# A sorted mixture-of-experts stage: its fp32 down product as three products of rounded halves

## The reference

```python
scores = sigmoid(x @ gate_w)                       # 32 experts
topk_w, topk_i = top_k(scores, 6); topk_w /= sum(topk_w)
combine = sum(one_hot(topk_i, 32) * topk_w[..., None], axis=1)
g = einsum('td,edf->tef', x, wg)                   # 256 -> 96 per expert
u = einsum('td,edf->tef', x, wu)
act = silu(g) * u
routed = einsum('tef,efd,te->td', act, wd, combine)  # 96 -> 256 per expert
```

## Time and profile before

| | us |
|---|---|
| median of three runs | 1384.87 (1383.31 to 1386.27) |
| span of the profiled execution | 1381.9 |
| TensorE busy | 1291.0 (93%) |
| ScalarE busy | 858.4 (62%) |
| VectorE busy | 844.4 (61%) |
| GpSimd busy | 617.0 (45%) |
| `sorted_tiles`: first transpose to last copy out | 608.6 to 955.1 |
| its down product, line 2018, 448 matmuls | 139.3 busy |

### The profile page before, as it was taken

How to read it: one execution, slowest core, us unless ns; L and a number is a source line. 1 busy time by engine, 2 the same in 40 slices (tenths; PEclk the granted TensorE clock), 3 DMA queues, 4 the chain that set the end, 5 groups by cost and what they waited for, 6 DMA issues and landing times. The chain is left out here.

```text
span 1381.9 us, 24599 instructions
## 1 busy us (share of the span) xinstructions
PE 1291.0 (93%) x7384; PEld 959.9 (69%) x7385; DVE 844.4 (61%) x3207; ACT 858.4 (62%) x2326; POOL 617.0 (45%) x542
## 2 busy tenths in 40 slices
PE   4999769999999999969999999997999999999997
PEld 3666446767777667757788888886667767777765
DVE  4587678777777677723333333333777777777774
ACT  1455427776677577635556656664777777777673
POOL 1111117777775777710000000001888888887820
PEclk9899979999999999999999999998999999999999
DMA  9977653333327422259976666664565665765510
GB/s 342 392 281 275 253 228 114 101 106 111 115 98 256 162 95 92 85 155 316 329 232 188 188 183 190 188 186 126 100 92 87 129 99 90 132 104 89 97 28 31
DMA packets 147284, 223.28 MB, mean 162 GB/s; under 512 B 13846, under 2 KB 128214, under 8 KB 142294
## 3 DMA queue, kind: packets, MB, share of 16 engines
q1 hardware_dynamic: 99350, 157.72, 33.9%
q0 software_dynamic: 36864, 53.50, 18.9%
q10 hardware_dynamic: 10944, 10.49, 2.6%
HBM read 105.27 MB, written 116.39 MB: 160 GB/s over the span
## 5 line engine op out<-in xcount | busy, mean ns | idle before, releaser
L1523 POOL DMA_INDIRECT l_sums<-sorted_y,slot_no x192 | 300.1, 1563 | 424.7 <-DMA l_sums<-base_dram 366.9
L1068 POOL DMA_INDIRECT sorted_x<-f_xn_row,slot_no x192 | 204.7, 1066 | 49.2 <-issue 44.5
L1224 ACT ACTIVATE f_prob<-f_prob,f_negmax 128x512 f32<-128x512 f32 (+3 forms) x256 | 142.6, 557 | 121.3 <-DVE f_negmax L1297 110.8
L2075 DVE SCALAR_TENSOR_TENSOR act_f<-hidden,rows_in,ps 128x96 f32<-128x96 f32 x224 | 70.5, 315 | 231.1 <-ACT hidden L2038 231.0
L1676 ACT ACTIVATE l_prob<-l_prob,l_negmax 128x512 f32<-128x512 f32 (+3 forms) x256 | 141.7, 555 | 104.9 <-DVE l_negmax L1760 97.2
L2000 PE MATMUL ps<-wgu_sb,xt_e 128*128 x896 | 184.2, 328 | 0.5 <-issue 0.4
L1565 PE MATMUL ps<-l_kt,l_qt 128*128 128x512 f32 (+3 forms) x512 | 170.5, 447 | 5.4 <-DVE l_qt L1751 4.8
L1127 PE MATMUL ps<-kt_s,f_qt 128*128 128x512 f32 (+3 forms) x512 | 170.8, 448 | 5.0 <-DVE f_qt L1288 4.4
L1297 DVE CUSTOM_DVE_ANT_0 f_prob<-ps,mask_add 128x512 f32<-128x512 f32 (+3 forms) x256 | 121.0, 486 | 83.5 <-issue 82.5
L1760 DVE CUSTOM_DVE_ANT_0 l_prob<-ps,mask_add 128x512 f32<-128x512 f32 (+3 forms) x256 | 121.0, 486 | 81.0 <-issue 79.7
L2000 PEld LDWEIGHTS ps<-wgu_sb,xt_e 128*128 128x128 f32 x896 | 139.9, 190 | 3.0 <-issue 2.0
(11 more groups left out here) (194 smaller groups left out, 2660.6 us busy)
## 6 DMA issues: line engine op xcount, KB each, us to landing
sorted_x<-zeros SPq DMA_DIRECT2D x14, 2304.0 KB, 9.8
rows_in<-sorted_x SPq DMA_DIRECT2D x112, 288.0 KB, 3.1
sorted_y<-rows_out SPq DMA_DIRECT2D x112, 256.0 KB, 2.1
wgu_sb<-in_wgu SPq DMA_DIRECT2D x16, 384.0 KB, 5.2
x_in<-in_x SPq DMA_DIRECT2D x8, 512.0 KB, 10.3
xn_dram<-xn SPq DMA_DIRECT2D x8, 512.0 KB, 4.0
base_dram<-x_in SPq DMA_DIRECT2D x8, 512.0 KB, 2.9
nqt_dram<-nqt_out SPq DMA_DIRECT2D x8, 512.0 KB, 3.9
```

The lines of the kernel that those rows point to most:

```text
L1068: pool.indirect_dma_start(sorted_x, bass.IndirectOffsetOnAxis(ap=slot_no[:, t, k:k + 1], axis=0), xn_row[buf][:], None).then_inc(scattered ...
L1224: act.activation(prob[:, i, qt, 0:w], prob[:, i, qt, 0:w], ACT.Exp, bias=negmax[:, i, qt:qt + 1], scale=-1.0, accum_out=rowsum[:, g // 2 % ...
L1523: pool.indirect_dma_start(sums[n % NSUM][:, t, :], None, sorted_y, bass.IndirectOffsetOnAxis(ap=slot_no[:, TT * GROUPS[n] + t, k:k + 1], a ...
```

## The change

The down product of line 2018 becomes `product3` on split halves. For that:

- `at` becomes a pair `at_hi`, `at_lo`. VectorE copies the turned activation to `at_hi` (rounded), waits for that copy on a semaphore of its own, and then subtracts: `at_lo` = PSUM - `at_hi`. `at_copied`, for which TensorE waits, is now counted up by the subtraction.
- The down weights become `wd_hi`, `wd_lo`. Chunks are loaded into two raw buffers in turn. VectorE splits chunk 0 at the start of the block, GpSimd splits chunks 1 to 7. The load of chunk n waits until raw buffer n%2 has been split. TensorE waits for the split of a chunk before the first down product that may use it.
- `ZCOLS`, the width of the zero tile from which `sorted_x` is cleared, is halved (each fill then reads it twice as often), and two small routing tensors live shorter. Both free SBUF.

```diff
-ZCOLS = 2304
+ZCOLS = 1152
...
-        sp.dma_start(self.wd[:, part, :], wd[:, part, :]).then_inc(self.chunk_loaded[n], 16)
+        sp.dma_start(self.wd_raw[n % 2][:], wd[:, part, :]).then_inc(self.wd_loaded[n % 2], 16)
...
                     if i == 0 and d % 2 == 0 and weights.EARLY + d // 2 < weights.CHUNKS:
-                        weights.load_chunk(sp, weights.EARLY + d // 2, wgu, wd)
+                        n = weights.EARLY + d // 2
+                        if n == 2:
+                            sp.wait_ge(wd_first, 1)
+                        else:
+                            sp.wait_ge(wd_split, n - 2)
+                        weights.load_chunk(sp, n, wgu, wd)
...
+        @block.gpsimd
+        def _(pool):
+            pool.wait_ge(wd_hi_made, 1)
+            for n in range(1, weights.CHUNKS):
+                part = slice(n * EACH, (n + 1) * EACH)
+                pool.wait_ge(wd_loaded[n % 2], 16 * (n // 2 + 1))
+                pool.tensor_copy(wd_s[0][:, part, :], wd_raw[n % 2][:]).then_inc(wd_hi_made, 1)
+                pool.wait_ge(wd_hi_made, n + 1)
+                pool.tensor_tensor(wd_s[1][:, part, :], wd_raw[n % 2][:], wd_s[0][:, part, :].bitcast(F32), ALU.subtract)\
+                    .then_inc(wd_split, 1)
...
-                        pe.matmul(y_ps[1 - par], at[1 - par][:],
-                                  wd_sb[:, bass.ds(owner, 1), :].rearrange("p a h -> p (a h)"), start=True, stop=True)\
+                        if c == 0:
+                            pe.wait_ge(wd_first, 1)
+                        elif c % EACH == 0 and c // EACH < weights.CHUNKS:
+                            pe.wait_ge(wd_split, c // EACH)
+                        product3(pe, y_ps[1 - par], [a[:] for a in at_s[1 - par]],
+                                 [w[:, bass.ds(owner, 1), :].rearrange("p a h -> p (a h)") for w in wd_s], True, True)\
                           .then_inc(y_ready, 1)
...
+            dve.wait_ge(wd_loaded[0], 16)
+            dve.tensor_copy(wd_s[0][:, 0:EACH, :], wd_raw[0][:]).then_inc(wd_hi_made, 1)
+            dve.wait_ge(wd_hi_made, 1)
+            dve.tensor_tensor(wd_s[1][:, 0:EACH, :], wd_raw[0][:], wd_s[0][:, 0:EACH, :].bitcast(F32), ALU.subtract)\
+               .then_inc(wd_first, 1)
...
                         dve.wait_ge(at_ready, c + 1)
-                        dve.tensor_copy(at[par][:], at_ps[par]).then_inc(at_copied, 1)
+                        dve.tensor_copy(at_s[par][0][:], at_ps[par]).then_inc(at_hi, 1)
+                        dve.wait_ge(at_hi, c + 1)
+                        dve.tensor_tensor(at_s[par][1][:], at_ps[par], at_s[par][0][:].bitcast(F32), ALU.subtract)\
+                           .then_inc(at_copied, 1)
```

More of the change, by code:

```diff
@@ L95, in build @@
         comb = sb("comb", [P, NT, NE])
-        slot_of = sb("slot_of", [P, NT, NE])
-        slot_top = sb("slot_top", [P, NT, 8])
         slot_no = sb("slot_no", [P, NT, TOPK], I32)
@@ L108, in build @@
                       xn_dram, base_dram, nqt_dram, nkv_dram, kt_dram, wq_dram, wvo_dram, rope_dram, sorted_x, tile_expert,
-                      comb, slot_of, slot_top, slot_no, ident, owner, owner_stored, mask, done, ps, weights, wgu, wd)
+                      comb, slot_no, ident, owner, owner_stored, mask, done, ps, weights, wgu, wd)
         with ExitStack() as ctx:
@@ L119, in attention @@
               xn_dram, base_dram, nqt_dram, nkv_dram, kt_dram, wq_dram, wvo_dram, rope_dram, sorted_x, tile_expert,
-              comb, slot_of, slot_top, slot_no, ident, owner, owner_stored, mask, done, ps, weights, wgu, wd):
+              comb, slot_no, ident, owner, owner_stored, mask, done, ps, weights, wgu, wd):
     def sb(name, shape, dt=F32):
@@ L148, in attention @@
     tile_c = latents(nc.sbuf_tensor("tile_c", [P, 1], F32))
+    slot_of = latents(nc.sbuf_tensor("slot_of", [P, NT, NE], F32))
+    slot_top = latents(nc.sbuf_tensor("slot_top", [P, NT, 8], F32))
     earlier = latents(nc.sbuf_tensor("earlier", [P, P], BF16))
@@ L855, in __init__ @@
         self.wgu = [whole.sb(f"wgu_sb{kc}", [P, NE, 2 * FE]) for kc in range(KC)]
-        self.wd = whole.sb("wd_sb", [FE, NE, H])
+        self.wd_hi = whole.sb("wd_hi", [FE, NE, H], F32R)
+        self.wd_raw = [ctx.enter_context(nc.sbuf_tensor(f"wd_raw{i}", [FE, self.EACH, H], F32)) for i in range(2)]
+        self.wd_loaded = [sem(f"wd_loaded{i}") for i in range(2)]
         self.rows_in = [ctx.enter_context(nc.sbuf_tensor(f"rows_in{i}", [P, 2, HW], F32)) for i in range(self.AHEAD)]
@@ L1896, in sorted_tiles @@
     AHEAD, EACH = weights.AHEAD, weights.EACH
-    rows_in, wgu_sb, wd_sb, expert_row = weights.rows_in, weights.wgu, weights.wd, weights.expert_row
+    rows_in, wgu_sb, expert_row = weights.rows_in, weights.wgu, weights.expert_row
     in_loaded, chunk_loaded, expert_loaded = weights.in_loaded, weights.chunk_loaded, weights.expert_loaded
     OUT = 4
+    wd_raw, wd_loaded = weights.wd_raw, weights.wd_loaded
+    wd_s = [weights.wd_hi, sb("wd_lo", [FE, NE, H], F32R)]
+    wd_hi_made, wd_first, wd_split = sem("wd_hi_made"), sem("wd_first"), sem("wd_split")
     rows_out = [sb(f"rows_out{i}", [P, 2, H]) for i in range(OUT)]
@@ L1903, in sorted_tiles @@
     act_f = [sb(f"act_f{i}", [P, FE]) for i in range(2)]
-    at = [sb(f"at{i}", [FE, P]) for i in range(2)]
+    at_s = [[sb(f"at_hi{i}", [FE, P], F32R), sb(f"at_lo{i}", [FE, P], F32R)] for i in range(2)]
     ALL_LAST = sum((NE - 1) << 8 * k for k in range(4))
@@ L1915, in sorted_tiles @@
     gu_ready, silu_done, act_done = sem("gu_ready"), sem("silu_done"), sem("act_done")
-    at_ready, at_copied = sem("at_ready"), sem("at_copied")
+    at_ready, at_hi, at_copied = sem("at_ready"), sem("at_hi"), sem("at_copied")
     y_ready, y_copied = sem("y_ready"), sem("y_copied")
@@ L1996, in steps @@
                         if c % EACH == 0 and c // EACH < weights.CHUNKS:
-                            pe.wait_ge(chunk_loaded[c // EACH], 16 * (KC + 1))
+                            pe.wait_ge(chunk_loaded[c // EACH], 16 * KC)
                         for kc in range(KC):
```

## The result

| | us |
|---|---|
| kernel after, median of 4 runs | 1400.48 (1399.87 to 1400.98) |
| kernel before, beside it, median of 4 | 1385.57 (1383.31 to 1386.49) |
| ratio, 95% interval | 1.0112 [1.0096, 1.0127] |
| span of the profiled execution | 1398.9 after 1381.9 |

The change costs 15 us in the timed runs and 17.0 us in the profiles. I had forecast 8.0 on the span, so the sign was right and the size was about half of what came. First the stage itself, busy time by stretch after the change; the row answers to the earlier trace rows.

A forecast was written before the change was run, and what follows sets the result against it. TensorE bounds the sorted experts' second part, hiding a loop by 0.02 us a tile; the loop takes over. Span 1381.9 + 4 (loop) + 2 (reads) + 2 (weights) = 1389.9, plus 3.0 to the median: 1393; range 1385 to 1403.

The forecast's parts named there:

- The loop: Sorted experts, 700 to 956 us: subtraction lengthens the two-tile round through the other engines from 2.79 to 3.03 us; +4 us.
- The reads: Sorted experts: TensorE's reads of expert numbers mostly hide in its new waiting; +2 us, bounds 0 and +13.7.
- the third row of the table: Stretch from copy out 65 to the last, 159 steps: forecast +5.5 us, from the +4 and +2 for 171 tiles.
- the reads stay on top of the loop: Rival, sorted experts: expert-number reads add fully to the longer round, 1.60 us a tile, +17.6, total 1404.5; chance 0.12.
- The zero tile: Fills that clear sorted_x, before the experts: halved width means more, shorter descriptors; forecast to cost nothing.
- That cover makes it nothing: Fills before the experts: GpSimd's scatter, waiting for them, ends 17 us before the first row is turned; cost 0.
- The weights: Start of the sorted experts: splitting weight chunks delays SyncE's chunk 2 by up to 2.2 us; +2, bounds 0 and +8.
- the first part: Sorted experts, 608 to 700 us, bound by DMA at 1.74 us a tile; the slower 1.52 us pace hidden there.
- the other estimate: GpSimd's copy when splitting a weight chunk: 0.9 us by the skill's line-rate rule, in place of 1.5.
- The halt of 3 us at chunk 4: SyncE, about 620.5 us: its queue waits 3 us for chunk 2's split, done by 623.5; issued transfers keep DMA busy.

The follow-up runs named there:

- the kernel with a cheaper read: Kernel after, with the expert-number word kept between iterations (one starting read, not two) and no range check, on TensorE and VectorE: 1394.53 against 1384.24, ratio 1.0077.
- before with the cheaper read: Kernel before, with the expert-number word kept between iterations (one starting read, not two) and no range check, on both engines: 1369.23 us, ratio 0.9905.
- the first kernel of that experiment: Kernel after, with the down product four steps behind the transposes, not three, four buffers per half, register reads unchanged: 1376.56 against 1384.24, ratio 0.9947.

## Why the prediction was right in sign and half in size

*The loop, right.* I forecast that the subtraction would make the loop of two tiles the bound, at 3.03 us. It is 3.05, in after's rounds without a read and in the kernel with a cheaper read. With the subtraction alone, and the fp32 pair kept, the same sum gives 3.11, and the run 3.13. TensorE alone would need 1.33, I said; with the product one step later it is 1.34. With the reads cheap the 159 steps go from 225.7 us (before with the cheaper read) to 243.0 (after with it), +17.3; the forecast's 1.52 - 1.41 over 159 steps is +17.5.

*The reads, the step that failed.* I wrote: "I take +2, near the first end, for the reads at the start of each iteration of 32 tiles, which come in pairs", and nothing for the single ones. In the last 159 steps the cheaper read takes 236.8 - 225.7 = 11.1 us off before and 247.84 - 242.97 = 4.9 off after. So the slack of the loop hides a good half of them. A single read costs 3.10 - 3.05 = 0.05 us where it cost 0.22; a pair at the start of an iteration costs 1.45 + 1.52 + 1.54 + 2.32 - 2 x 3.05 = 0.73, where it cost 0.8: hidden hardly at all. My reason for hiding was that steps need not be even. That holds for a single read behind a gate/up product, and I had no row for one ahead of it, as at an iteration's start. That the pair is too long for the wait is not shown: with one read in that place alone the first four tiles cost 1.0 to 1.1 us over two rounds. The other half of this miss is in the base. I counted the reads of before at (1.497 - 1.41) x 159 = 13.8 us; they were 11.1, since 256/171 charges the stretch's edges to its tiles (from copy to copy it is 236.8/159 = 1.489) and the plain step is 1.417. Together (13.8 - 11.1) + (4.9 - 1.9) = 5.7, less the 0.2 by which the forecast of the loop was too high: the 5.5 that the third row of the table lacks.

*The rival "the reads stay on top of the loop"* asked for all 13.7 us; 6.7 of 13.4 stayed over the whole stage. That counts what the cheaper read takes off, not all that the reads cost. The truth lay about halfway, inside the bounds of 0 and 13.7, and my value of 2 was too near the first.

*The zero tile, wrong.* "That cover makes it nothing" priced the transfers, which were and are hidden, and not their issue. It is SyncE's time that doubles, in a block that ends with SyncE: +3.6 us in the profile, 3.1 in the run of it alone. I had the row of GpSimd's memset and never looked at SyncE's row of the same fills, although the prediction itself counts SyncE's delays elsewhere.

*The weights, right in number and mostly by luck.* +2 forecast for the splits and nothing for the slower loop, which I took to be hidden behind DMA in the first part. +2.95 measured, of which at most 1.3 goes with the splits and most comes from the subtraction in each tile: without it and with the splits the first part is no longer than before. SyncE issued chunk 2 1.8 us after the first turned row, before 0.2 us ahead of it; so 2.0 where I had 2.2. GpSimd's chunks take 1.03 + 2.36 + the gap, 3.5 us, where I took 4; the copy is nearer to the 0.9 that I had as the other estimate than to my 1.5. The halt of 3 us at chunk 4 did not come: its split ended at 624.58 and SyncE issued the chunk at 624.61, 0.18 us behind its last issue where such a gap is 0.04 otherwise. Starts on SyncE, GpSimd and VectorE:

```profile
614.05 0.82 SPq L880 DMA_DIRECT2D wgu_sb<-in_wgu  x2
...
624.61 0.83 SPq L880 DMA_DIRECT2D wgu_sb<-in_wgu  x2
```
```profile
612.83 2.09 POOL L1980 CAST wd_hi<-wd_raw 96x1024 fp32r<-96x1024 f32 x1 [9.55 <-DVE wd_hi L2080]
615.00 2.35 POOL L1982 TENSOR_TENSOR wd_lo<-wd_raw,wd_hi 96x1024 fp32r<-96x1024 f32 x1
621.11 1.03 POOL L1980 CAST wd_hi<-wd_raw 96x1024 fp32r<-96x1024 f32 x1 [3.76 <-DMA wd_raw<-in_wd]
622.22 2.36 POOL L1982 TENSOR_TENSOR wd_lo<-wd_raw,wd_hi 96x1024 fp32r<-96x1024 f32 x1
```
```profile
612.80 1.22 DVE L2082 TENSOR_TENSOR wd_lo<-wd_raw,wd_hi 96x1024 fp32r<-96x1024 f32 x1
```

The first copy on GpSimd takes 2.09 us beside VectorE's subtraction of 1.22, each of the next six 1.03: it lost 1.06 us beside the 1.22. The Trainium skill, SBUF — State Buffer, § Who interferes with whom, has such a pair exclude each other, and this trace agrees. It was GpSimd that waited, whose instruction started 0.03 us later, so SyncE's chunk 2 was not held by it.

The step of the prediction that failed is thus two terms of its sum: the reads, sized at +2 on a base that was too high, which lack 5.5 us, and the zero tile at nothing, which lacks 3.6. The sum of what I missed: 3.6 (fills) + 5.5 (reads and their base) + 0.95 (first part) - 0.6 (behind the stage) = 9.45, of the 17.0 - 8.0 = 9.0 us; the 0.5 over is the 12 tiles by which the two countings of the stage's later part differ.

## What to carry to other kernels

Ask of each added microsecond whether it lies in the engine or in the loop: splitting a product saved TensorE 0.08 us a tile and cost the loop 0.32 us a round, and one more step of distance, with twice the buffers, turned a loss of 1.1% into a gain of 0.5%. When a change makes DMA pieces smaller, price their issue on the queue that issues them, and see whether a block ends there. A run-time register read belongs where its engine has a wait to spare, and without checks that a mask makes needless: with one read fewer an iteration that edit gave 1% to 1.3% in the fp32 kernel, more than the three products gave. Give the kernel before the same edits before crediting a gain to one of them.

## What the runs showed of the hardware

- The issue of a fill with twice as many pieces of half the length is not twice as long but stalls in places: 0.59, 2.48, 1.35 and 4.96 us for four in a row, where the longer pieces took 0.68 to 1.45. Three of the shorter kind end at 24.9 us, four of the longer at 24.6.
- TensorE's register read takes 0.30 us at its quickest and 0.6 in the median of before. With the product one step later, in the first kernel of that experiment, it is 0.30 throughout:

```profile
L1995 PEldq TENSOR_LOAD <-expert_row x47: 296/301/315, 702.6 to 936.1; - x47
```

  What it waits for in the other case is not shown by a run.
- Register arithmetic stands behind the wait of the instruction that uses it, in this kernel. Silu ends at 780.33 and the scaled product begins at 780.63: in these 0.3 us VectorE's queue has three register instructions of line 2105, two of 0.045 us and one of 0.057, with which it works out an address. It lies in the loop before and after; working it out ahead of the wait was not tried.
